# The head of a decoder layer: projections wait by weight quarter, the second chunk's queries and keys in front of the first's values, products of zeros in front, masks loaded last

## The chip, the cores and the metric

The kernel runs on one core of one Trainium2 chip. The time is that of the device for one execution, in microseconds (us); the measurement before is the median of three runs, 813.57 us (811.46 to 815.69). The engines are TensorE (PE in the profile; PEld is its weight load), VectorE (DVE), ScalarE (ACT), GpSimd (POOL) and SyncE (SP, which only issues DMAs here). A name with a q behind it (ACTq, SPq) is the instruction stream of that engine when it issues a DMA.

## The reference

A decoder layer in three blocks, each followed by a layer norm over `x + block(x)`, for 4 sequences of 512 tokens and 512 features. The first block, where the change lies, is linear attention:

```python
q = (x @ Wq).reshape(B, T, H, D)          # B = 4, T = 512, H = 16, D = 32, E = 512
k = (x @ Wk).reshape(B, T, H, D)
v = (x @ Wv).reshape(B, T, H, D)
q, k = _rotary(q), _rotary(k)
# chunks of 128 tokens: inter = (q * q_decay) @ kv, scores = (q @ k^T) * dmask, out = inter + scores @ v
attn = _rms_norm(attn, rms_w)             # x * rsqrt(mean(x * x) + eps) * w
return attn @ Wo
```

The second block is an int8-quantised gated product of each sequence with given weights, the third a gated feed-forward block whose weights are 4-bit codes with fp16 scales, decoded in the kernel.

## The kernel before, in words

**Tiling.** The 2048 tokens are 16 chunks of 128 (`CHUNKS`, four to a sequence). The attention block goes chunk by chunk. For chunk n: the tokens' features are transposed (`xT`, four 128x128 transposes on TensorE, L1266), projected to queries, keys and values (`q`, `k`, `v`, each one PSUM bank of 128x512), queries and keys are rotated by GpSimd (`rotate`), transposed per head group (`qT`, `kT`, L1302), the scores of 16 heads are formed (`s0` to `s3`, L1317), masked by VectorE (L1197), multiplied by the values (`attn`, L1345), and projected by Wo (`y`, L1362).

**Two parts per number.** Each float32 operand of a projection is split into a rounded part (`hi`, written by ScalarE) and the rest (`lo`, written by VectorE), and a product is three matmuls: hi with lo, hi with hi, lo with hi. So a projection of one chunk is 4 quarters (k = 0 to 3, 128 rows of the weight each) of 3 matmuls, 12 matmuls of 128x512 (L1278). The weights' own split happens once, at the head: `weight_hi(p)` on ScalarE (L959) and `weight_lo(p)` on VectorE (L1146), four instructions for each of Wq, Wk, Wv and Wo (p = 0 to 3). Each `lo` adds one to the semaphore `w_ready`. Wo is first multiplied by the norm's weights `rms_col` on VectorE (L1231), for which both must have landed (`wo_in`).

**Order.** Every engine has its own program, a list of instructions carried out in order, and waits on semaphores. The order of the uses of a PSUM bank is written out in `attention_order()`; q, k and v of chunk 0 lie in banks 2, 3 and 0, those of chunk 1 in the same banks after them. The streams at the head:

- SyncE issues x of chunk 0, the first halves of Wq and Wk, the table, the first half of Wv, the masks, the scales of the feed-forward weights, the packed words (`load_words(0)`, three DMAs, L896), then waits until all of Wo is split (`w_ready` at 16) and loads later inputs (L886, L913, L882).
- ScalarE first issues the identity, the second halves of Wq and Wk, x of chunk 1, the second half of Wv, all of Wo, and `rms_col`. Then it computes, in this order: `x_hi(0)`, `weight_hi(0)`, (1), (2), q and k of chunk 0 copied out of PSUM (`projected(0, 0)`, `projected(0, 1)`, L968), `x_hi(1)`, `projected(0, 2)`, `weight_hi(3)`, an fp16 identity (`ident16`, L1047), the scales' columns (L1049), and `chunk(0)`, which begins with q and k of chunk 1 and then `kT_hi` and `qT_hi`.
- VectorE: four small memsets, `x_lo(0)`, `weight_lo(0)`, (1), (2), `x_lo(1)`, the four multiplications of Wo, `weight_lo(3)`, then a wait for the table and the masks, and the chunks.
- TensorE: the transposes of chunk 0, then for p = 0 to 2 a wait until all four quarters of that weight are split and 12 matmuls, with the transposes of chunk 1 behind p = 1. Then `chunk(0)`: q of chunk 1, two fp16 transposing products of the scales that need `ident16` (`scale_columns`, L1288), k of chunk 1, the transposes of rotated q and k, the scores, and so on.
- GpSimd: rotates chunk 0 when its q and k have been copied out, writes the decayed keys `kd` of that chunk, then the same for chunk 1.

Of the kernel before, what the change touches and what calls it, by code (L numbers as in the profile page):

```python
# [19 lines left out]
P = 128  # L20
B, T, E = 4, 512, 512
NC = T // P
NK = E // P
H, D = 16, 32
HG = P // D
NG = H // HG
# [572 lines left out]
def attention_order():  # L599

    def pieces(n, place):
        return (("piece", m - len(PIECES)) for m in PIECES_AT.get((n, place), ()) if PIECE_BANKS[m] < 6)

    yield from (("xT", 0), ("q", 0), ("k", 0), ("xT", 1), ("v", 0), ("q", 1), ("k", 1))
    for n in range(CHUNKS):
        yield from (("qT", n), ("kT", n))
        if n > 0:
            yield from (("q", n + 1), ("k", n + 1))
        yield from (("s0", n), ("s1", n), ("s2", n), ("s3", n))
        if n % NC < NC - 1:  # L610
            yield ("kv", n)
        yield ("v", n + 1)
        yield from pieces(n, "masks")
        yield from (("attn", n), ("xT", n + 2))
        yield from pieces(n, "split")
        yield from (("y", n), ("ss", n))
        yield from pieces(n, "end")
# [144 lines left out]
def attention_programs(nc, sem, a, memory, expert, weights, x1, x2_v, x2_stored):  # L762
# [22 lines left out]
    z_first_loaded, z_loaded = sem("z_first_loaded"), sem("z_loaded")  # L785
    x1_first_stored, x1_stored = weights.x1_first_stored, weights.x1_stored
    words_in, bits_done, values_done = sem("words_in"), sem("bits_done"), sem("values_done")
    packed = sem("packed")
    ident_in, ident16_set, scales_in, scale_ps, cols_set = (sem("ident_in"), sem("ident16_set"), sem("scales_in"),
                                                            sem("scale_ps"), sem("cols_set"))  # L790
    wo_scaled = sem("wo_scaled")
# [88 lines left out]
    def sync_program(sp):  # L880
# [13 lines left out]
        def load_words(b):  # L894
            for dst, src in packed_words(b):
                sp.dma_start(dst, src).then_inc(words_in, 16)  # L896
# [3 lines left out]
        load_half(sp, 1, w_k, 0)  # L900
        sp.dma_start(tab[:, :], table[:, 2 * P:TABLE_W]).then_inc(tab_in, 16)
        load_half(sp, 2, w_v, 0)
        sp.dma_start(mask[:, :, :, :], masks.rearrange("p (j g c) -> p j g c", j=HG, g=NG)).then_inc(mask_in, 16)
        gu_rows, dn_rows = scale_rows[0:SCALES[0], 0, :], scale_rows[0:SCALES[1], 1, :]
        sp.dma_start(gu_rows, a["L0_ffn_gate_up_scales"].rearrange("g (t p) -> (g t) p", p=P)).then_inc(scales_in, 16)
        sp.dma_start(dn_rows, a["L0_ffn_down_scales"].rearrange("g (t p) -> (g t) p", p=P)).then_inc(scales_in, 16)
        load_words(0)
        sp.wait_ge(w_ready, 4 * NK)
        load_z(0, True)
        load_z(0, False)  # L910
# [29 lines left out]
    def scalar_program(act):  # L940
# [4 lines left out]
        load_half(act, 1, w_k, 1)  # L945
        act.dma_start(x_in[:, 1, :], x_v[0][:, 1, :]).then_inc(x_loaded[1], 16)
        load_half(act, 2, w_v, 1)
        act.dma_start(raw[:, 3], w_o.rearrange("(k p) n -> p k n", p=P)).then_inc(wo_in, 16)
        act.dma_start(rms_col[:, :], rms_w.rearrange("(k p) -> p k", p=P), allow_slow_non_contiguous=True)\
            .then_inc(wo_in, 16)  # L950

        def weight_hi(n):
            for k in range(NK):
# [7 lines left out]
        def x_hi(n):  # L961
            wait_full(act, "xT", n)
            nc.scalar.activation(xT_hi[:, n % 2], in_groups("xT", n), ACT.Copy).then_inc(xT_hi_done, 1)

        def projected(n, p):
            u = "qkv"[p]
            wait_full(act, u, n)
            nc.scalar.activation(qkv[:, n % 2, p * E:(p + 1) * E], bank(u, n)[:, :], ACT.Copy)\  # L968
                .then_inc(drain_sem(u, n), 1)
# [25 lines left out]

        def chunk(n):
            b, c = divmod(n, NC)
            if n == 0:
                projected(1, 0)
                projected(1, 1)  # L1000
            wait_full(act, "kT", n)
            nc.scalar.activation(kT_hi[:, :, :], in_groups("kT", n), ACT.Copy).then_inc(kT_hi_done, 1)
            wait_full(act, "qT", n)
# [33 lines left out]
        x_hi(0)  # L1037
        weight_hi(0)
        weight_hi(1)
        weight_hi(2)  # L1040
        projected(0, 0)
        projected(0, 1)
        x_hi(1)
        projected(0, 2)
        weight_hi(3)
        act.wait_ge(ident_in, 16)
# [72 lines left out]
    def vector_program(dve):  # L1119
# [58 lines left out]
        def chunk(n):  # L1178
# [41 lines left out]
            if n < CHUNKS - 1:  # L1220
                beside_pieces(weights.lo, dve, n, "end")

        expert.set_biases()
        x_lo(0)
        weight_lo(0)
        weight_lo(1)
        weight_lo(2)
        x_lo(1)
        dve.wait_ge(wo_in, 32)
        for k in range(NK):  # L1230
            nc.vector.tensor_scalar(raw[:, 3, k, :], raw[:, 3, k, :], rms_col[:, k:k + 1], None,  # L1231
# [16 lines left out]
    def tensor_program(pe):  # L1248
        steps = expert.tensor_steps(pe)

        def passes(lh, ll, rh, rl):

            return (lh, rl), (lh, rh), (ll, rh)
# [16 lines left out]
        def project(n, p, ks=range(NK)):  # L1270
            u = "qkv"[p]
            if ks[0] == 0:
                start_use(u, n)
                wait_drained(pe, "xT", n)
            for k in ks:
                for m, (lhs, rhs) in enumerate(passes(xT_hi[:, n % 2, k, :], xT_lo[:, n % 2, k, :],
                                                      wqkv_hi[:, p, k, :], wqkv_lo[:, p, k, :])):
                    last = nc.tensor.matmul(bank(u, n)[:, :], lhs, rhs, start=(k == 0 and m == 0),  # L1278
                                            stop=(k == NK - 1 and m == 2))
            if ks[-1] == NK - 1:  # L1280
                last.then_inc(full[BANK_OF[u]], 1)

        def scale_columns():
            pe.wait_ge(ident16_set, 1)
# [7 lines left out]
        def chunk(n):  # L1292
            c = n % NC
            if n == 0:
                project(1, 0)
                scale_columns()
                project(1, 1)
            pe.wait_ge(rot_done, 2 * (n + 1))
            for p, u in enumerate(("qT", "kT")):
                filled = start_use(u, n)  # L1300
# [69 lines left out]
            beside(steps, n, 2)  # L1370
            beside_pieces(weights.product, pe, n, "end")

        pe.wait_ge(ident_in, 16)
        transpose_x(0)
        for p in range(3):
            pe.wait_ge(w_ready, (p + 1) * NK)
            project(0, p)
            if p == 1:
                transpose_x(1)
        for n in range(CHUNKS):  # L1380
            chunk(n)

# [389 lines left out]
```

## Time and profile before

| | |
|---|---|
| median of 3 runs | 813.57 us (811.46 to 815.69) |
| the profiled execution's own time | 815.23 us |
| its span in the profile | 813.4 us |
| granted TensorE clock, mean | 0.961 |
| TensorE busy | 734.4 us (90%) |
| VectorE, ScalarE, GpSimd busy | 473.2, 354.7, 201.1 us |

The span runs from the first to the last instruction; the other 1.8 us of that execution's time lie around it. The profile rows give the start, the duration, engine, line and operation, then written tile `<-` read tiles, the shape and how many instructions are merged (`x4`); in brackets stands the idle time of the engine just before, and what ended it. TensorE's matmuls are pipelined, so a row's duration runs into the next row: what one costs in a series is the distance between two starts. The granted clock is given as a share of 2.4 GHz. In the first 12 us its column reads 1.00, though the distances there are those of 1.2 GHz.

### The profile page before, as it was taken

Reading aid. Unit: us, or ns where it says so; the run is one execution under the profiler, and the core shown is the slowest. Engines: PE = TensorE matmul, PEld = TensorE weight load, DVE = VectorE, ACT = ScalarE, POOL = GpSimd, SP = SyncE. Lnnn points to the kernel's source line nnn. Section 1 sums busy time; section 2 is a strip of 40 time slices with the busy share of each in tenths; the row PEclk is TensorE's granted clock in tenths of the full one; section 3 lists DMA queues with packets and bytes.
Section 4 is the critical chain, followed back from the end, with each engine's and each line's share of the span. In section 5 each row is a group of like instructions: output and inputs, shape, how many; then the busy total and the mean of one; then the engine's idle time right before and its main releaser. Section 6 shows DMA issues by size and latency. Waiting matters only on the chain.

```text
span 813.4 us, 11711 instructions
## 1 busy us (share of the span) xinstructions
PE 734.4 (90%) x4662; PEld 590.3 (73%) x4662; DVE 473.2 (58%) x911; ACT 354.7 (44%) x566; POOL 201.1 (25%) x235
## 2 busy tenths in 40 slices
PE   5898899998999898579899999999998999999992
PEld 4677678877887686358687777877777877788881
DVE  4566768783568656776625468655568454633214
ACT  4344454347453552462533463545364625522212
POOL 0444344344443459821201100211001111000000
PEclk9899999999999999759999999999999999999996
DMA  9400100102200220040001130030120030100201
GB/s 323 181 15 1 53 1 17 38 2 77 100 21 1 94 76 1 1 154 2 2 26 52 52 104 0 1 130 0 52 104 0 27 104 1 52 0 1 104 0 53
DMA packets 25408, 41.18 MB, mean 51 GB/s; under 512 B 5002, under 2 KB 7690, under 8 KB 25226
## 3 DMA queue, kind: packets, MB, share of 16 engines
q1 hardware_dynamic: 23194, 37.40, 13.5%
q10 hardware_dynamic: 2160, 3.02, 1.1%
q8 instruction: 38, 0.62, 0.3%
q14 instruction: 16, 0.13, 0.1%
HBM read 28.88 MB, written 11.53 MB: 50 GB/s over the span
## 4 chain that ended last, share of the span: by engine, by line
PE 59%; DVE 24%; ACT 10%; issue 2%; DMA 2%; POOL 1%; ACTq 0%; DVEq 0%; POOLq 0%
PE ps L1589 22%; PE ps L1278 11%; PE ps L1603 10%; PE ps L1362 3%; DVE small L413 3%; PE ps L1317 3%; PE ps L525 3%; PE ps L534 2%; DMA rms_col<-in_L_attn_rms_w_dram 2%; DVE masked L1197 2%; DVE w L406 2%; DVE act_s L374 2%; DVE act_s L406 1%; DVE weights L738 1%; PE ps L1345 1%
## 5 line engine op out<-in xcount | busy, mean ns | idle before, releaser
L1589 PE MATMUL ps<-x2T_hi,weights 128*128 128x512 f32 x704 | 220.0, 394 | 0.0
L1589 PEld LDWEIGHTS ps<-x2T_hi,weights 128*128 128x128 f32 x704 | 134.1, 191 | 27.9
L1589 PE MATMUL ps<-x2T_lo,weights 128*128 128x512 f32 x352 | 143.0, 406 | 0.8 <-DVE x2T_lo L1522 0.8
L1532 DVE TENSOR_TENSOR silu<-ps,silu 128x512 f32<-128x512 f32 x44 | 30.3, 689 | 147.5 <-PE ps L1589 147.5
L1603 PE MATMUL ps<-weights,h_hi 128*128 128x512 f32 x352 | 111.1, 397 | 1.8 <-DVE h_lo L1516 1.8
L1278 PE MATMUL ps<-wqkv_lo,xT_hi 128*128 128x512 f32 x192 | 81.9, 427 | 10.7 <-DVE wqkv_lo L1146 5.0
L1589 PEld LDWEIGHTS ps<-x2T_lo,weights 128*128 128x128 f32 x352 | 67.1, 191 | 15.1 <-DVE x2T_lo L1522 1.2
L1460 ACT ACTIVATE silu<-ps 128x512 f32<-128x512 f32 x44 | 26.3, 597 | 118.6 <-PE ps L1589 118.6
L1278 PE MATMUL ps<-wqkv_hi,xT_lo 128*128 128x512 f32 x192 | 77.1, 402 | 0.0
L1278 PE MATMUL ps<-wqkv_hi,xT_hi 128*128 128x512 f32 x192 | 77.1, 401 | 0.0
L1603 PEld LDWEIGHTS ps<-weights,h_hi 128*128 128x128 f32 x352 | 64.5, 188 | 15.1 <-DVE h_lo L1516 2.5
L1074 POOL TENSOR_TENSOR rot<-qkv,tab 128x256 f32<-128x256 f32 x64 | 44.7, 733 | 121.3 <-ACT qkv L968 121.3
L1454 ACT ACTIVATE h_hi<-silu 128x512 fp32r<-128x512 f32 x44 | 27.8, 631 | 103.0 <-DVE silu L1532 103.0
L1603 PE MATMUL ps<-weights,h_lo 128*128 128x512 f32 x176 | 68.7, 390 | 0.0
L338 POOL TENSOR_SCALAR act_s<-act_s 128x1024 f32<-128x1024 f32 (+1 forms) x16 | 13.3, 830 | 183.3 <-ACT act_s L276 183.2
L1197 DVE TENSOR_TENSOR masked<-ps,mask 128x512 f32<-128x512 f32 x64 | 39.7, 683 | 28.9 <-PE ps L1317 28.9
L1278 PEld LDWEIGHTS ps<-wqkv_lo,xT_hi 128*128 128x128 f32 x192 | 37.2, 194 | 21.7 <-DVE wqkv_lo L1146 5.4
L1516 DVE TENSOR_TENSOR h_lo<-silu,h_hi 128x512 fp32r<-128x512 f32 x44 | 30.6, 696 | 37.4 <-ACT h_hi L1454 37.4
L968 ACT ACTIVATE qkv<-ps 128x512 f32<-128x512 f32 x48 | 28.6, 596 | 53.4 <-PE ps L1278 53.3
L1278 PEld LDWEIGHTS ps<-wqkv_hi,xT_lo 128*128 128x128 f32 x192 | 37.3, 194 | 8.6
L1278 PEld LDWEIGHTS ps<-wqkv_hi,xT_hi 128*128 128x128 f32 x192 | 37.3, 194 | 6.4
L1603 PEld LDWEIGHTS ps<-weights,h_lo 128*128 128x128 f32 x176 | 33.0, 188 | 7.2
(170 smaller groups left out, 1357.5 us busy)
## 6 DMA issues: line engine op xcount, KB each, us to landing
w<-in_fside_BxS2xS_dram SPq DMA_DIRECT2D x4, 1024.0 KB, 5.3
x_dram<-xb SPq DMA_DIRECT2D x4, 1024.0 KB, 4.3
xc<-x_dram SPq DMA_DIRECT2D x4, 1024.0 KB, 5.5
x_in<-in_x_dram SPq DMA_DIRECT2D x15, 256.0 KB, 3.4
xb<-x_dram SPq DMA_DIRECT2D x3, 1024.0 KB, 5.6
out_dram<-xc SPq DMA_DIRECT2D x3, 1024.0 KB, 4.7
z<-in_x_dram SPq DMA_DIRECT2D x3, 768.0 KB, 5.2
x_dram<-z SPq DMA_DIRECT2D x3, 768.0 KB, 3.5
```

What stands on the lines that cost most here:

```text
L406: step = nc.vector.tensor_tensor(act_s[:, c, 0:width] if use[0] in "xa" else src[:, c, 0:width], src[:, c, 0:width], self.bank(use)[:, 0:w ...
L413: then_wait(nc.vector.tensor_reduce(small[:, slot, :], src[:, :, 0:width], AX.X, ALU.max, apply_absolute_value=True))
L968: nc.scalar.activation(qkv[:, n % 2, p * E:(p + 1) * E], bank(u, n)[:, :], ACT.Copy)\
L1074: nc.gpsimd.tensor_tensor(rot[:, m], v, f, ALU.mult).then_inc(rot_a, 1)
L1197: nc.vector.tensor_tensor(masked[:, j], in_groups(f"s{j}", n), mask[:, j], ALU.mult)\
L1278: last = nc.tensor.matmul(bank(u, n)[:, :], lhs, rhs, start=(k == 0 and m == 0), stop=(k == NK - 1 and m == 2))
L1454: nc.scalar.activation(h_hi[:, it % 2, :], silu[:, it % 2, :], ACT.Copy).then_inc(h_hi_done, 1)
L1460: nc.scalar.activation(silu[:, it % 2, :], ps[4][:, :], ACT.Silu).then_inc(silu_done, 1)
L1516: nc.vector.tensor_tensor(h_lo[:, it % 2, :], silu[:, it % 2, :], h_hi[:, it % 2, :].bitcast(F32), ALU.subtract).then_inc(h_lo_done, 1)
L1532: nc.vector.tensor_tensor(silu[:, it % 2, :], ps[5][:, :], silu[:, it % 2, :], ALU.mult)\
L1589: last = nc.tensor.matmul(dst[:, :], lhs, rhs, start=(k == 0 and n == 0), stop=(k == NK - 1 and n == 2))
L1603: last = nc.tensor.matmul(ps[c][:, :], lhs, rhs, start=(it == 0 and n == 0), stop=(it == NI - 1 and n == 2))
```

## The change

It has five parts, all at the head.

1. TensorE's first projections wait quarter by quarter (`w_ready` at p * 4 + k + 1 in front of quarter k), for chunk 0 alone.
2. q and k of chunk 1 are projected in front of v of chunk 0, on TensorE, in the order of bank uses and on ScalarE; ScalarE's split of Wv goes behind `x_hi(1)`, VectorE's `x_lo(1)` in front of `weight_lo(2)`.
3. VectorE sets one half of `kd` (128x512) to zero first of all; TensorE multiplies its columns by one another, 14 times in front of the transposes of chunk 0 and 10 times behind them, into a bank that nothing reads (`turn_over`).
4. The loads of Wo and `rms_col` go from ScalarE's stream to SyncE's, in the place of the masks.
5. The load of the masks goes behind the packed words.

```diff
-    yield from (("xT", 0), ("q", 0), ("k", 0), ("xT", 1), ("v", 0), ("q", 1), ("k", 1))
+    yield from (("xT", 0), ("q", 0), ("k", 0), ("xT", 1), ("q", 1), ("k", 1), ("v", 0))
@@ sync_program
         load_half(sp, 2, w_v, 0)
-        sp.dma_start(mask[:, :, :, :], masks.rearrange("p (j g c) -> p j g c", j=HG, g=NG)).then_inc(mask_in, 16)
+        sp.dma_start(raw[:, 3], w_o.rearrange("(k p) n -> p k n", p=P)).then_inc(wo_in, 16)
+        sp.dma_start(rms_col[:, :], rms_w.rearrange("(k p) -> p k", p=P), allow_slow_non_contiguous=True)\
+            .then_inc(wo_in, 16)
...
         load_words(0)
+        sp.dma_start(mask[:, :, :, :], masks.rearrange("p (j g c) -> p j g c", j=HG, g=NG)).then_inc(mask_in, 16)
@@ scalar_program
         load_half(act, 2, w_v, 1)
-        act.dma_start(raw[:, 3], w_o.rearrange("(k p) n -> p k n", p=P)).then_inc(wo_in, 16)
-        act.dma_start(rms_col[:, :], rms_w.rearrange("(k p) -> p k", p=P), allow_slow_non_contiguous=True)\
-            .then_inc(wo_in, 16)
...
         def chunk(n):
             b, c = divmod(n, NC)
-            if n == 0:
-                projected(1, 0)
-                projected(1, 1)
...
         weight_hi(1)
-        weight_hi(2)
         projected(0, 0)
         projected(0, 1)
         x_hi(1)
+        weight_hi(2)
+        projected(1, 0)
+        projected(1, 1)
         projected(0, 2)
         weight_hi(3)
@@ vector_program
+        nc.vector.memset(kd[:, 1, :], 0.0).then_inc(zeros_set, 1)
         expert.set_biases()
         x_lo(0)
         weight_lo(0)
         weight_lo(1)
+        x_lo(1)
         weight_lo(2)
-        x_lo(1)
@@ tensor_program
             for k in ks:
+                if n == 0:
+                    pe.wait_ge(w_ready, p * NK + k + 1)
...
+        def turn_over(times):
+
+            for _ in range(times):
+                nc.tensor.matmul(ps[7][:, 0:P], kd[:, 1, 0:P], kd[:, 1, P:2 * P], start=True, stop=True)
...
             if n == 0:
-                project(1, 0)
                 scale_columns()
-                project(1, 1)
...
+        pe.wait_ge(zeros_set, 1)
+        turn_over(14)
         pe.wait_ge(ident_in, 16)
         transpose_x(0)
-        for p in range(3):
-            pe.wait_ge(w_ready, (p + 1) * NK)
-            project(0, p)
-            if p == 1:
-                transpose_x(1)
+        turn_over(10)
+        project(0, 0)
+        project(0, 1)
+        transpose_x(1)
+        project(1, 0)
+        project(1, 1)
+        project(0, 2)
```

## Rows read from the trace of the kernel before

**Rows 1.** The page: busy time and share of TensorE, VectorE, ScalarE, GpSimd.

```profile
PE 734.4 (90%) x4662; PEld 590.3 (73%) x4662; DVE 473.2 (58%) x911; ACT 354.7 (44%) x566; POOL 201.1 (25%) x235
```

**Rows 2.** Chain of waits, 3 to 25 us: start, duration, what.

```profile
3.85 16.96 DMA rms_col<-in_L_attn_rms_w_dram
...
20.83 3.51 DVE raw L1231 x4
...
24.36 0.63 ACT wo_hi L959
```

**Rows 3.** TensorE in order of time, 4 to 32 us.

```profile
4.34 1.11 PE L1266 MATMUL ps<-ident_ones,x_in 128*128 128x128 f32 x4 [4.34 <-DMA ident_ones<-in_table_dram]
10.50 0.79 PE L1278 MATMUL ps<-wqkv_lo,xT_hi 128*128 128x512 f32 x1 [5.05 <-DVE wqkv_lo L1146]
...
15.35 0.40 PE L1278 MATMUL ps<-wqkv_hi,xT_lo 128*128 128x512 f32 x1
...
18.32 0.60 PE L1266 MATMUL ps<-ident_ones,x_in 128*128 128x128 f32 x4
18.67 0.48 PE L1278 MATMUL ps<-wqkv_lo,xT_hi 128*128 128x512 f32 x1
...
24.00 0.39 PE L1278 MATMUL ps<-wqkv_hi,xT_lo 128*128 128x512 f32 x1
25.25 0.34 PE L1288 MATMUL ps<-sq 88*128 88x88 f16 x2 [0.86 <-ACT sq L1047]
...
28.39 1.03 PE L1302 MATMUL ps<-ident_ones,qkv 128*128 128x128 f32 x8
31.70 0.34 PE L1317 MATMUL ps<-qT_lo,kT_hi 32*128 32x128 f32 x4 [2.27 <-DVE qT_lo L1184]
```

**Rows 4.** ScalarE in order of time, 3 to 28 us, and 362 to 368 us.

```profile
3.85 1.55 ACTq L949 DMA_DIRECT2D rms_col<-in_L_attn_rms_w_dram  x1
5.43 1.28 ACT L963 ACT_TABLE_LOAD   x1 [5.43 <-issue]
6.72 0.60 ACT L963 ACTIVATE xT_hi<-ps 128x512 fp32r<-128x512 f32 x1
7.22 2.18 ACT L959 ACTIVATE wqkv_hi<-raw 128x512 fp32r<-128x512 f32 x4
...
362.77 1.28 ACT L1460 ACT_TABLE_LOAD   x1
367.34 0.60 ACT L1460 ACTIVATE silu<-ps 128x512 f32<-128x512 f32 x1 [3.29 <-PE ps L1589]
```

**Rows 5.** VectorE in order of time, 0 to 31 us.

```profile
0.81 0.15 DVE L258 MEMSET biases<- 128x1 f32 x4 [0.81 <-PEq L1758]
...
7.96 5.08 DVE L1146 TENSOR_TENSOR wqkv_lo<-raw,wqkv_hi 128x512 fp32r<-128x512 f32 x8
```

**Rows 6.** SyncE's stream, 4 to 28 us.

```profile
4.61 9.93 SPq L896 DMA_DIRECT2D halves<-_ffn_gate_up_packed_dram  x3
```

**Rows 7.** TensorE in order of time: products of 128x128 at either clock.

```profile
33.86 2.08 PE L1326 MATMUL ps<-qkv,kd 128*128 128x128 f32 x8
35.59 0.77 PE L1278 MATMUL ps<-wqkv_lo,xT_hi 128*128 128x512 f32 x1
...
52.62 1.16 PE L1326 MATMUL ps<-qkv,kd 128*128 128x128 f32 x8
53.53 0.48 PE L1278 MATMUL ps<-wqkv_lo,xT_hi 128*128 128x512 f32 x1
...
325.50 2.08 PE L1338 MATMUL ps<-qdT,kv 128*128 128x128 f32 x8
...
357.64 3.65 PE L1621 MATMUL ps<-ident_ones,xb 128*128 128x128 f32 x16 [1.87 <-DVE weights L738]
```

**Rows 8.** Stretches: us, length, busy of the five engines, granted clock, DMA share, GB/s.

```profile
32.30:39.10 6.80, 6.80 (x66) 5.60 (x65) 3.08 (x5) 0.00 (x0) 2.32 (x3) 0.51 1.02 381
...
329.00:330.00 1.00, 0.99 (x18) 0.45 (x8) 0.00 (x0) 0.49 (x1) 1.00 (x2) 0.82 0.00 0
```

More of the change, by code:

```diff
@@ L787, in attention_programs @@
     words_in, bits_done, values_done = sem("words_in"), sem("bits_done"), sem("values_done")
-    packed = sem("packed")
+    packed, zeros_set = sem("packed"), sem("zeros_set")
     ident_in, ident16_set, scales_in, scale_ps, cols_set = (sem("ident_in"), sem("ident16_set"), sem("scales_in"),
```

## The prediction

> **What bounds the kernel now.** I read the page's first part, then the chain of waits, then each engine in order of time over the first 40 us, because all edits lie there. The first shows TensorE busy for 90% of the span with no other engine above 58% [rows 1]: outside the head TensorE carries the time, and whatever the head gains or loses is handed on nearly whole. The chain begins with the load of `rms_col`, which follows that of Wo and is in after 20.81 us; then come the multiplications of Wo on VectorE, the split of Wo on ScalarE, the fp16 identity, and the scales' products on TensorE at 25.25 [rows 2, 3]. On TensorE I mark three losses. It does nothing but four transposes before 10.50, where the first projection had waited 5.05 us for the whole split of Wq. From 10.50 to about 15.2 a matmul of 128x512 costs 0.43 us, which is 1.2 GHz; from 15.35 on 0.23, which is 2.4 GHz. And it stands for 0.86 us in front of the scales' products [rows 3]. The mark I measure by is the start of the transposes of rotated q and k at 28.39 [rows 3]: all that the change reorders lies in front of it, and from it on the programs are the same.
>
> **The first projection.** The zeroing is put in front of VectorE's first instruction at 0.81 [rows 5]. No row shows a memset of 128x512; the nearest are the memset of 128x1, 0.15 us, and the split of 128x512, 5.08 / 8 = 0.64 [rows 5]. I take 0.6, since the size decides, so products begin at about 1.5 (1.0 to 1.6). A float32 product of 128x128 costs (35.59 - 33.86) / 4 = 0.43 us at 1.2 GHz and (53.53 - 52.62) / 4 = 0.23 at 2.4 [rows 7]. Fourteen are 6.0 us at the low clock, more than the 2.8 us left until the identity lands at 4.34 [rows 3], so they delay the transposes. How much depends on when the clock rises. Before, it rose some 4.7 us after the first projection [rows 3]; the same distance here gives 6.2. By then (6.2 - 1.5) / 0.43 = 10.9 products are done, the other 3.1 take 0.7: 6.9. The transposes end at 7.5 (0.60 us as at 18.32 [rows 3]) instead of 5.45.
>
> ScalarE was not ready at 5.45 either: its stream issued DMAs until 5.40, then loaded its table for 1.28, and `xT_hi` began at 6.72 [rows 4]. Two of those DMAs leave its stream (1.55 for `rms_col` and about 0.55 for Wo), so the table load can begin at about 3.3. Does it run before the wait for TensorE is over? At 362.77 it did: the load ran at once and its activation waited 3.29 us more [rows 4]. So it ends at 4.6, hidden, and `xT_hi` starts at 7.55, which is 0.83 later than before; were it not hidden, 1.28 more. The first quarter of Wq's `lo` came 7.96 + 0.64 - 6.72 = 1.88 after `xT_hi` [rows 4, 5], thus at 9.45. The ten products behind the transposes run from 7.25 to 9.6. First projection: **9.6** instead of 10.50, all at the high clock.
>
> Do the waits by quarter cost or bring anything? VectorE delivers a quarter every 0.64 us [rows 5], TensorE needs 3 x 0.232 = 0.70 (23 distances in the 5.33 us from 18.67 to 24.00 [rows 3]), so behind the first quarter none is waited for; the waits earn only that the first matmul starts behind the first quarter, not the fourth, and that is inside the 9.6. The last quarter of Wk is there at 13.9 and wanted at 14.5.
>
> **From there to the mark.** q and k of chunk 0: 24 matmuls at the high clock, 5.55, end at 15.15 (before: 7.82 us, of which 2.27 are lost to the low clock [rows 3]). Transposes of chunk 1: 0.35, until 15.5. Now q of chunk 1 stands next, and it needs `xT_lo` of chunk 1: behind the copy of k (from 15.35, 0.5), `xT_hi` (0.65) and `xT_lo` (0.7) it is there at 17.25. Before, v of chunk 0 filled that gap; now TensorE waits **1.75 us**. Wv's split behind it is in time: ScalarE from 16.35 to 18.5, VectorE to about 19.7, wanted at 22.8. Three projections, 36 x 0.23 = 8.3, end at **25.55**.
>
> Here the gain is lost. ScalarE copies v of chunk 0 only now (25.75), and `weight_hi(3)` stands behind that copy in its list. Before, that copy ran at 21.7, and the Wo split was limited by the landing [rows 2]. Now the landing is no limit: the products of Wo by `rms_col` would be done by about 24.3 even with the landing at 20.8, yet the split runs from 26.25, four times 0.53 (rate of Wq's, 2.18 for four with overlap [rows 4]), to 28.35; the fp16 identity is ready so that the scales' products start at 28.7 (0.89 after the start of the last split, 24.36 to 25.25 [rows 2, 3]), after a wait of 3.15 us. With 0.26 for them the mark is at **28.96, 0.57 later** than 28.39. Check by differences: start -0.9, low clock -2.27, new gap +1.75, last wait 3.15 instead of about 1.0 (24.23 to 25.25) +2.15, rest -0.15: +0.6.
>
> Bounds of this part: a rise of the clock at 4.9 lets the products end early and the first projection come at about 9.0, mark at +0.0; a rise only at 8.9 moves the transposes' end to 8.6 and the first projection to 10.9, mark at +1.8; a table load that isn't hidden, +1.1.
>
> **The clock behind the mark.** Before, TensorE stood from 29.4 to 31.70, its clock fell at 32.3 and rose at 39.1, so 6.8 us passed at half speed [rows 3, 8]. Now, from 25.55 to the scores at about 32.3, it has 0.26 us of products and 1 us of transposes. The clock falls again, and probably earlier: the 8 transposes then take 1.86 instead of 0.93 and the scores 2.6 instead of 2.2. I add **0.9**, between nothing and 1.3, and keep 3 more us at the high end for a second such stretch.
> What the trace shows of transposes: sixteen filled 3.65 us from 357.64 on and the clock stayed at 0.5 [rows 7]. The Trainium skill, TensorE: Matmul & The Clock Gate, Part 4 (PE-mode transpose), says that transposes don't count as busy for the clock gate. By that rule nearly the whole 6.7 us count as idle and the sum is the one above; were they to count, the 0.9 would go. The trace agrees with the rule.
>
> **What costs nothing.** The masks are issued behind the packed words, whose three issues last until 14.5 [rows 6], somewhat later with 1.55 us for `rms_col` and the 0.5 for Wo ahead. VectorE waits for the masks in front of `kT_lo`, at about 30.8; the bytes of the head are the same, and were all in at 20.8 [rows 2], so some 9 us cover it. SyncE's wait for `w_ready` ends some 1.5 us later, with it the loads behind; the transposes of chunk 2 that need x are 1.5 later as well. GpSimd rotates chunk 0 some 3 us earlier and chunk 1 some 6 us earlier, and neither was waited for.
>
> **Sum.** 0.57 + 0.9 = +1.5 on the execution of 815.23 us: 816.7. That one lies 1.7 above the median of the runs, 813.57, to which I add the same: **815.1 us**.
>
> **Rivals.**
> *The products of zeros don't raise the clock.* For it: from 32.3 to 35.7 TensorE was full with scores and four such products and stayed low to 39.1 [rows 7, 8]. Against: the clock rose near 329.2 after such products from 325.50 on and small ones behind them, with none of 128x512 in 5 us before [rows 7, 8]. Then all 24 run at 0.43 with slow transposes between: 1.5 + 6.0 + 1.1 + 4.3 = 12.9 for the first projection, +2.4; no low clock is saved, 0; gap and last wait +1.75 + 2.15, rest -0.15: +6.2, with 0.9 behind the mark +7.1: **820.7 us**. It decides from the point where fewer than half of the products run at the high clock. Chance 0.14.
> *The clock doesn't fall behind the mark.* The 6.8 us [rows 8] would shrink: scores 0.7, `kd` products 0.8, six projection matmuls 1.4, values 0.3, together 3.2, against +0.6: -2.6, **811.0 us**. Against it speaks the long idle before the scores. Chance 0.12.
> *The wait for Wo stays as before.* If DMAs in SyncE's stream land Wo after 25 us, the multiplications (3.51 [rows 2]) set the split: every us beyond 22.7 costs one. A landing at 25 gives +2.3 more, **817.4 us**. The queue behind it held back three issues for 9.9 us [rows 6], Wo stands in front of them. Chance 0.06.
>
> **How the numbers follow.** My forecast holds 0.68. Range: from 811.0, the case in which the clock stays, to 819.5, past the late-rise and late-Wo cases and part of the way to 820.7. 0.5% is 4.1 us, about what a measurement of this kernel tells from no change (three runs spread over 4.2). Faster by more needs the clock to stay and a lucky early rise: 0.07. Slower by more: the zeros rival and a part of the others, 0.17. Within: 0.76.
>
> **What would show it.** Right: first L1278 near 9.6 and starts 0.23 apart at once; a gap of some 1.7 us in front of q of chunk 1; L1288 at 28 to 29.5 behind ScalarE's split of Wo, which starts behind the copy of v; transposes at 29 to 30; half clock from before 32. Wrong: L1288 without a wait, or transposes before 27, would mean that the gain isn't eaten; starts 0.43 apart beyond 12 us, that the zeros don't work; a `masked` that waits for the masks, that the cover in the DMA part is gone.

## The result, and the profile after

| | before | changed |
|---|---|---|
| median, 16 runs each | 814.86 us (811.46 to 817.48) | 817.71 us (815.94 to 821.01) |
| ratio to before, 95% interval | | 1.0040 (1.0025 to 1.0054) |
| profiled execution, its span | 815.23, 813.4 us | 817.66, 815.8 us |
| granted clock of that execution, mean | 0.961 | 0.955 |

The change makes the kernel slower by 0.4%, some 3 us, less than the 0.5% that I had named as the bound, though with 16 runs of each the interval lies wholly above 1. The forecast was 815.1 us (811.0 to 819.5), a rise of 1.5. So the measured 817.71 lies inside the range and 2.6 us above its middle: 1.3 us of that because the kernel before is at 814.86 over 16 runs, not at the 813.57 of the three runs that I started from, and the other 1.3 because the rise was some 3 us and not 1.5.

TensorE of the changed kernel in order of time, columns as in [rows 3]. L1288 are the products of zeros (28 records for 14 products), L1280 the projections (before L1278), L1295 the scales' products, L1307 the transposes of queries and keys, L1322 the scores:

```profile
1.45 4.91 PE L1288 MATMUL ps<-kd 128*128 128x128 f32 x28 [1.45 <-DVE kd L1222]
6.20 0.60 PE L1266 MATMUL ps<-ident_ones,x_in 128*128 128x128 f32 x4
6.64 2.40 PE L1288 MATMUL ps<-kd 128*128 128x128 f32 x20
8.90 0.47 PE L1280 MATMUL ps<-wqkv_lo,xT_hi 128*128 128x512 f32 x1
...
14.47 0.60 PE L1266 MATMUL ps<-ident_ones,x_in 128*128 128x128 f32 x4
16.62 0.47 PE L1280 MATMUL ps<-wqkv_lo,xT_hi 128*128 128x512 f32 x1 [1.55 <-DVE xT_lo L1149]
...
24.66 0.39 PE L1280 MATMUL ps<-wqkv_hi,xT_lo 128*128 128x512 f32 x1
28.00 0.34 PE L1295 MATMUL ps<-sq 88*128 88x88 f16 x2 [2.96 <-ACT sq L1046]
28.27 1.73 PE L1307 MATMUL ps<-ident_ones,qkv 128*128 128x128 f32 x8
32.34 0.48 PE L1322 MATMUL ps<-qT_lo,kT_hi 32*128 32x128 f32 x4 [2.33 <-DVE qT_lo L1183]
```

From top to bottom: the first projection starts 1.60 us earlier than in [rows 3]; queries and keys of chunk 0 are done 3.85 us earlier (14.47 against 18.32); then come two holes, 1.55 us in front of the queries of chunk 1, and 2.96 us in front of the scales' products; the mark, the transposes of queries and keys, stands at 28.27 against 28.39. Of 3.85 us there are 0.12 left. The second hole is explained by ScalarE's list:

```profile
22.36 0.60 ACT L968 ACTIVATE qkv<-ps 128x512 f32<-128x512 f32 x1 [2.12 <-PE ps L1280]
25.08 0.60 ACT L968 ACTIVATE qkv<-ps 128x512 f32<-128x512 f32 x1 [2.12 <-PE ps L1280]
25.57 2.18 ACT L959 ACTIVATE wo_hi<-raw 128x512 fp32r<-128x512 f32 x4
27.65 0.30 ACT L1046 ACTIVATE sq<-ident_ones 128x128 f16<-128x128 f32 x1
```

The second row is the copy of the values of chunk 0. ScalarE waits 2.12 us for it with nothing to do, and only then splits Wo, for which everything had been ready since 24.2 (the multiplications by `rms_col` run on VectorE from 20.75 for 3.42 us).

Stretches of the changed kernel, columns as in [rows 8]; the first answers to the low stretch there:

```profile
28.00:39.00 11.00, 8.66 (x72) 7.64 (x72) 7.02 (x10) 1.37 (x3) 1.43 (x2) 0.53 0.66 231
39.00:62.00 23.00, 20.81 (x202) 16.75 (x200) 14.20 (x31) 9.13 (x12) 9.31 (x11) 1.00 0.19 63
62.00:70.00 8.00, 5.91 (x18) 4.80 (x19) 5.43 (x12) 5.23 (x7) 2.78 (x3) 0.57 0.00 0
70.00:103.00 33.00, 30.38 (x293) 25.17 (x290) 21.37 (x42) 11.02 (x17) 12.52 (x16) 1.00 0.12 30
103.00:108.00 5.00, 3.82 (x11) 3.07 (x12) 3.52 (x11) 3.56 (x5) 1.80 (x2) 0.66 0.06 21
```

and three of these of the kernel before:

```profile
28.00:39.00 11.00, 8.73 (x85) 7.20 (x87) 4.37 (x7) 1.68 (x3) 5.21 (x7) 0.70 0.92 332
62.00:70.00 8.00, 6.70 (x28) 5.59 (x29) 5.92 (x13) 5.57 (x9) 2.79 (x3) 0.79 0.00 0
103.00:108.00 5.00, 5.00 (x29) 4.26 (x28) 2.80 (x8) 4.14 (x6) 1.80 (x2) 1.00 0.00 0
```

The granted clock (the third number from the end) is lower in three places: 0.53 for 0.70, 0.57 for 0.79, 0.66 for 1.00. The way of the loss: 0.12 us ahead at the mark, 0.64 behind at the scores (32.34 against 31.70), 0.79 at Wo's product of chunk 0 (42.45 against 41.66), 1.79 at the transposes of chunk 2's queries (69.59 against 67.80), 3.09 at those of chunk 4 (108.50 against 105.41), 2.4 at the end of the span.

### The profile page after: what moved, and what is told of

Same layout as the page of the kernel before. It is cut to its first block, busy times and chain, and to the rows that moved or that the text cites. A ratio compares the mean times of both kernels' runs of the same rounds, so it can differ in the third digit from the quotient of the medians.

```text
span 815.8 us, 11808 instructions
## 1 busy us (share of the span) xinstructions
PE 741.7 (91%) x4710; PEld 598.0 (73%) x4710; DVE 476.3 (58%) x912; ACT 354.4 (43%) x566; POOL 203.2 (25%) x235
## 4 chain that ended last, share of the span: by engine, by line
PE 60%; DVE 24%; ACT 10%; issue 2%; POOL 1%; DMA 1%; SPq 0%; DVEq 0%; ACTq 0%; POOLq 0%
PE ps L1598 22%; PE ps L1280 12%; PE ps L1612 10%; PE ps L1367 3%; DVE small L413 3%; PE ps L525 2%; PE ps L1322 2%; PE ps L534 2%; DVE masked L1196 2%; DVE w L406 2%; DVE act_s L374 1%; DVE act_s L406 1%; DVE weights L738 1%; DVE e_stats L459 1%; ACT values_gu L980 1%
## 5 line engine op out<-in xcount | busy, mean ns | idle before, releaser
L1280 PE MATMUL ps<-wqkv_lo,xT_hi 128*128 128x512 f32 x192 | 80.8, 421 | 7.2 <-ACT rms L1029 2.8
L1280 PE MATMUL ps<-wqkv_hi,xT_lo 128*128 128x512 f32 x192 | 76.1, 397 | 0.0
L1280 PE MATMUL ps<-wqkv_hi,xT_hi 128*128 128x512 f32 x192 | 76.0, 396 | 0.0
L1280 PEld LDWEIGHTS ps<-wqkv_lo,xT_hi 128*128 128x128 f32 x192 | 36.6, 191 | 17.8 <-issue 4.7
L1280 PEld LDWEIGHTS ps<-wqkv_hi,xT_lo 128*128 128x128 f32 x192 | 36.6, 191 | 8.4
L1280 PEld LDWEIGHTS ps<-wqkv_hi,xT_hi 128*128 128x128 f32 x192 | 36.8, 192 | 6.3
```

## The experiments

Each kernel was timed beside the kernel before on the same chip, in three series of four (e1 to e4, e5 to e8, e9 to e12), each series on another chip, with 5 to 12 runs for each kernel and 23 to 28 of the kernel before. The changed kernel was not timed again in them; its row is from the result above. "Mark" is the start of the transposes of queries and keys of chunk 0, "y" that of Wo's product of chunk 0, in the one profiled execution. The profiled executions of e1 and e3 are quicker than their medians (811.67 and 806.91 us); I read positions in the head from them, no times. A position moves between executions too: up to the mark the kernel before and e5 differ only by two small loads that nothing waits for there, and their marks are 0.9 us apart (28.39 and 29.29), so a difference of less than a microsecond at the mark or at y says little. The median of the kernel before was 814.94, 816.43 and 816.11 us in the three series, so ratios are compared across them, not medians.

| kernel | median us | ratio to before (95%) | mark | y |
|---|---|---|---|---|
| changed | 817.71 | 1.0040 (1.0025 to 1.0054) | 28.27 | 42.45 |
| e1: Wo's split ahead | 816.03 | 1.0011 (0.9984 to 1.0037) | 25.89 | 40.63 |
| e2: without products of zeros | 820.65 | 1.0074 (1.0046 to 1.0101) | 30.97 | 46.55 |
| e3: old order of projections | 813.14 | 0.9979 (0.9958 to 1.0000) | 26.00 | 37.55 |
| e4: e1 and 8 products behind the mark | 819.72 | 1.0063 (1.0042 to 1.0085) | 26.10 | 41.98 |
| e5: before, x loaded early | 815.76 | 0.9985 (0.9970 to 1.0000) | 29.29 | 40.95 |
| e6: e1, x loaded early | 816.16 | 0.9991 (0.9977 to 1.0006) | 26.45 | 40.25 |
| e7: e3, x loaded early | 811.58 | 0.9936 (0.9920 to 0.9952) | 25.60 | 37.29 |
| e8: e4, x loaded early | 813.42 | 0.9954 (0.9940 to 0.9968) | 26.21 | 38.92 |
| e9: e7 and the 8 products | 810.71 | 0.9943 (0.9918 to 0.9969) | 25.41 | 35.76 |
| e10: before, new loads alone | 813.94 | 0.9979 (0.9960 to 0.9997) | 26.93 | 39.96 |
| e11: e9 and 14 products in chunk 1 | 807.27 | 0.9892 (0.9860 to 0.9924) | 25.91 | 36.26 |
| e12: e7, one wait per weight | 812.50 | 0.9956 (0.9937 to 0.9976) | 27.14 | 38.88 |

**Is it the place of Wo's split (e1)?**

```diff
-        projected(0, 2)
         weight_hi(3)
         act.wait_ge(ident_in, 16)
         nc.scalar.activation(ident16, ident, ACT.Copy).then_inc(ident16_set, 1)
+        projected(0, 2)
```

> The changed kernel with one thing moved: ScalarE's split of Wo and the fp16 identity in front of its copy of v of chunk 0. My theory (the gain of the head is lost because that split stands behind the copy of v): no wait of 3 us in front of the scales' products, transposes of q and k at 25.4 instead of 28.3, scores of chunk 0 at 28.8 instead of 32.3, the time 3 us below the changed kernel's, so about level with the kernel before or 0.5 under it. Rival (the loss lies behind the mark, in the clock, and takes whatever the head gives): transposes at 25.4 too, but the values' part of chunk 0 as late as in the changed kernel and its time as well, 817 to 818.

```profile
25.31 0.34 PE L1295 MATMUL ps<-sq 88*128 88x88 f16 x2 [0.25 <-ACT sq L1045]
25.89 1.06 PE L1307 MATMUL ps<-ident_ones,qkv 128*128 128x128 f32 x8 [0.24 <-ACT qkv L968]
30.14 0.48 PE L1322 MATMUL ps<-qT_lo,kT_hi 32*128 32x128 f32 x4 [3.19 <-DVE qT_lo L1183]
...
40.22 0.66 PE L1266 MATMUL ps<-ident_ones,x_in 128*128 128x128 f32 x4 [0.96 <-DMA x_in<-in_x_dram]
```

At the mark the theory holds: 0.25 us of wait instead of 2.96, and the mark 2.38 us earlier. The time followed by 1.7 us, not 3, and the ratio's interval overlaps that of the changed kernel: by itself the time doesn't settle it. The rows show where the rest stays. The wait in front of the scores grew from 2.33 to 3.19, because VectorE is busy with the rest of Wo's split when `kT_hi` is ready. And TensorE now waits for x of chunk 2, which it did not in the kernel before.

**Do the products of zeros pay (e2)?** Part 3 is left out: `turn_over`, its calls and the memset.

> The changed kernel without the 24 products of zeros and without the zeroing. Theory (the products pay for themselves by the clock, 2.3 us, and cost part of that by delaying the transposes and the first projection): first projection at 7.9 instead of 8.9 but 0.43 us a matmul until about 12.5, projection of k of chunk 0 done at 15.8 instead of 14.6, transposes of q and k at 29.5 instead of 28.3, time +1 us against the changed kernel. Rival (the products are a net loss): projection of k done before 14.6 and the time lower by 1 us.

Without them k of chunk 0 ended 2.67 us later (17.14 against 14.47) and so did the mark, 2.70. The median is 2.9 us higher, more than the 1 us that I expected. The two intervals overlap a little (1.0046 to 1.0101, and 1.0025 to 1.0054), but six of the seven runs without the products lie above 15 of the 16 with them. I had the first projection at 7.9 where it came at 8.69: the split of Wq waits for its landing until 7.19, so without the products it is that landing that bounds the start, and the delay of the transposes by the products cost only 0.2 us. So they lose next to nothing of what the clock brings. How much that is, is partly chance: here the low clock lasted 6.1 us from the first projection, in [rows 3] 4.7.

**Is it the order of projections (e3)?** Part 2 is undone on all engines, the rest of the change is kept.

> The changed kernel with the order of projections of the kernel before on all engines (v of chunk 0 in front of q and k of chunk 1, the split of Wv in front of the copies, the split of Wo between them), with waits by quarter, zeros and new load order kept. Theory (the new order of projections is what costs): v of chunk 0 fills the gap of 1.55 us in front of q of chunk 1, the scales' products wait less than 1 us, transposes of q and k at 25.5, time 3 us below the changed kernel's. Rival (the order costs nothing, the loads or the clock do): transposes near 28 and the time that of the changed kernel.

```profile
14.50 0.60 PE L1267 MATMUL ps<-ident_ones,x_in 128*128 128x128 f32 x4
15.78 0.47 PE L1281 MATMUL ps<-wqkv_lo,xT_hi 128*128 128x512 f32 x1 [0.68 <-DVE wqkv_lo L1146]
...
22.87 0.34 PE L1296 MATMUL ps<-sq 88*128 88x88 f16 x2 [1.12 <-ACT sq L1047]
26.00 1.03 PE L1310 MATMUL ps<-ident_ones,qkv 128*128 128x128 f32 x8
29.30 0.33 PE L1325 MATMUL ps<-qT_lo,kT_hi 32*128 32x128 f32 x4 [2.27 <-DVE qT_lo L1184]
```

Two holes of 4.5 us together are now two of 1.8 (0.68 and 1.12), the mark is 2.27 us earlier, the scores 3.04. The ratio falls from 1.0040 to 0.9979 with intervals apart: **the new order costs 0.6%, about 4.6 us** (817.71 less 813.14, with the two medians of before 0.1 apart), and the other four parts together are worth 0.2%, with an interval that touches 0. Here the theory and the time agree.

**Is the idle behind the mark what drops the clock (e4)?**

```diff
+        def hold(times):
+            for _ in range(times):
+                nc.tensor.matmul(ps[7][:, 0:P], ident, ones, start=True, stop=True)
...
                 step.then_inc(filled, 1)
+            if n == 0:
+                hold(8)
```

> The first of these (Wo's split ahead of the copy of v), and 8 products of identity by ones behind the transposes of q and k of chunk 0, where TensorE stands for 2.3 us until the scores. Theory (transposes don't count for the clock and the wait behind them does, so the clock falls in front of the scores): the clock stays high through the scores and values of chunk 0, which saves 2 to 3 us more: values of chunk 0 done 5 to 6 us earlier than in the changed kernel, time 5 us below it. Rival (the fall has another cause, or it is chance of the moment): half clock from the scores on all the same, and the time that of the first, plus up to 1 us where the products run at half clock and delay the scores.

A miss: the slowest but one. The first two rows below went as I wanted, eight products in the idle and the scores at the high clock (their groups 0.11 us apart). But the clock fell all the same, only later: the stretch from 32.6 to 35.8 has a granted clock of 0.50, so the low stretch behind the mark is 3.4 us long where it was 6.8 in e1. The last row shows the price:

```profile
27.00 1.95 PE L1292 MATMUL ps<-ident_ones 128*128 128x128 f32 x16
30.37 0.33 PE L1328 MATMUL ps<-qT_lo,kT_hi 32*128 32x128 f32 x4 [1.42 <-DVE qT_lo L1183]
35.82 1.12 PE L1356 MATMUL ps<-masked,qkv 128*32 128x128 f32 x32
41.57 0.66 PE L1266 MATMUL ps<-ident_ones,x_in 128*128 128x128 f32 x4 [3.03 <-DMA x_in<-in_x_dram]
```

TensorE arrives 2 us sooner and waits 3.03 us for x of chunk 2. Soon behind that wait, from 42.8 on, its clock is low again, and Wo's product takes 4.4 us (41.98 to 46.40) instead of 2.8 in e1. SyncE's list shows why x is late: five loads of 3 MB together stand before it, and those wait for Wo's split.

```profile
28.99 0.81 SPq L886 DMA_DIRECT2D xb<-in_x_dram  x2
29.84 0.96 SPq L886 DMA_DIRECT2D z<-in_x_dram  x2
30.84 0.49 SPq L916 DMA_DIRECT2D w<-in_fside_BxS2xS_dram  x1
31.38 11.21 SPq L882 DMA_DIRECT2D x_in<-in_x_dram  x3
```

**Is x of chunk 2 the next limit (e5 to e8)?** Four kernels get the same edit. It does two things: x of chunks 2 and 3 is loaded in front of SyncE's wait for the split of Wo, and the second sequence's residual loads (`load_z(1, ...)`) wait until the first's have landed. No run has one without the other:

```diff
+        for n in range(2):
+            wait_full(sp, "xT", n)
+            load_x(n + 2)
         sp.wait_ge(w_ready, 4 * NK)
         load_z(0, True)
         load_z(0, False)
-        load_z(1, True)
-        load_z(1, False)
         sp.dma_start(expert.w[:, :, :], w_rows[0]).then_inc(expert.w_in, 16)
+        sp.wait_ge(z_first_loaded, 16)
+        sp.wait_ge(z_loaded, 16)
+        load_z(1, True)
+        load_z(1, False)
...
             if n + 2 < CHUNKS:
-                wait_full(sp, "xT", n)
-                load_x(n + 2)
+                if n >= 2:
+                    wait_full(sp, "xT", n)
+                    load_x(n + 2)
```

> The kernel before with x of chunks 2 and 3 loaded as soon as their buffers are read, in front of SyncE's wait for the split of Wo, and the second sequence's residual loads behind the first's landing. In the trace of the kernel before nothing waited for x of chunk 2, so by my theory (this load is a limit only once the head is quicker than in the kernel before) the time is that of the kernel before within 1 us. Rival (the load order costs in every case): 1 to 2 us less.

> The changed kernel with Wo's split ahead of the copy of v, and the early loads of x of chunks 2 and 3. Theory (x of chunk 2, issued behind the split of Wo and five large loads, is the next limit): the wait of 0.96 us for it is gone, the transposes of the second chunk's queries at 42.6 instead of 43.6, time 1 us below that of the kernel with Wo's split ahead alone (816.0). Rival (that wait only stood beside another of the same length): both marks as there, time 816.

> The changed kernel with the old order of projections, and the early loads of x. Theory as in the one before: the wait of 1.0 us for x of chunk 2 gone, transposes of the second chunk's queries at 39.6 instead of 40.5, time 1 us below the old order's 813.1, so some 812, 3 us under the kernel before. Rival: 813.

> The kernel with Wo's split ahead and 8 products of identity by ones behind the transposes, with the early loads of x. Without them it was slower (819.7) than its twin without products (816.0), and in its trace TensorE waited 3.03 us for x of chunk 2 and ran at half clock for 3.4 us behind that wait. Theory (the products do hold the clock; the time that they gain ends at x of chunk 2, and the wait there drops the clock again): the wait and the half clock at 42 to 46 are gone, transposes of the second chunk's queries at 41 instead of 46.5, time near 814, 5 us below 819.7. Rival (the products themselves cost the time): 819 again.

None of the four waits for x of chunk 2. In the kernel before (e5) it brought at most 0.3%, with an interval that touches 1. With Wo's split ahead (e6) no clear gain, though y is 0.4 earlier in an execution whose first projection was 0.55 later: 0.9991 against 1.0011, intervals overlapping. With the old order (e7) the ratio went from 0.9979 to 0.9936, intervals just apart, and with the products (e8) from 1.0063 to 0.9954: a loss of 0.6% turned into a gain of 0.5%. Against e6, its twin without the 8 products in the same series, e8 is 2.7 us quicker with the intervals apart. So the products behind the mark are worth something, and in e4 the late loads took it and more. As in e4, they shorten the low stretch behind the mark (3.4 us in e8, 6.8 in e6) and don't remove it. Rows of e8, in order of time:

```profile
27.12 1.95 PE L1298 MATMUL ps<-ident_ones 128*128 128x128 f32 x16
30.57 0.33 PE L1334 MATMUL ps<-qT_lo,kT_hi 32*128 32x128 f32 x4 [1.50 <-DVE qT_lo L1189]
38.56 0.60 PE L1272 MATMUL ps<-ident_ones,x_in 128*128 128x128 f32 x4
...
41.89 1.07 PE L1317 MATMUL ps<-ident_ones,qkv 128*128 128x128 f32 x8
```

**What the parts are worth, and what they give together (e9 to e12).** e9 is e7 with the 8 products; e10 the kernel before with parts 4 and 5 alone; e12 is e7 with the waits of the kernel before in place of part 1; e11 is e9 with this:

```diff
             beside_pieces(weights.product, pe, n, "split")
+            if n == 1:
+                hold(14)
```

> The changed kernel with the old order of projections, the early loads of x, and 8 products of identity by ones behind the transposes of chunk 0's queries and keys. It joins what gained alone (old order with early loads 811.6; products with the split of Wo ahead 813.4 against 816.2 without them). Theory (they act in different places: the order at the mark, the products on the clock behind it): no low clock between 20 and 55 us, time 2 us below the old order's with early loads, so near 809.5. Rival (the old order leaves so short an idle that the clock's fall there costs nothing): 811.5.

> The kernel before with the new places of the loads alone: Wo and rms_col in SyncE's stream in the masks' place, the masks behind the packed words. Theory (Wo lands some 3 us earlier, the split of Wo and the identity are done sooner, the wait of 0.86 us in front of the scales' products goes, and the first copy starts 1.2 us earlier because ScalarE's stream is shorter): first projection at 9.3 to 10.5, transposes of queries and keys at 26.5 to 27.5 instead of 28.4, time 1 to 2 us below the kernel before. Rival (the loads give nothing, since a wait for one thing is replaced by the next): transposes at 28.4 and the time of before.

> The kernel with old order, early loads and 8 products, and 14 more products of identity by ones in front of Wo's product of chunk 1, where TensorE waits 4.2 us for VectorE and ScalarE. Theory (the idle of 4.2 us is what drops the clock at 60 us, for 3.4 to 6.8 us): no low clock before 95 us, transposes of the third chunk's queries 4.5 us behind y of chunk 1's start in low-clock traces become 3 us, time 1.5 to 2.5 us below its twin without the 14. Rival (the clock falls all the same, or the products delay Wo's product): the same time or 1 us more.

> The changed kernel with old order and early loads, but with one wait per weight, as in the kernel before, instead of one per quarter. Theory (VectorE delivers a quarter each 0.64 us, TensorE needs 0.70, so the quarters save what lies between the first and the fourth quarter minus what the products of zeros hide): first projection 1.0 to 1.5 us later, transposes of queries and keys later by that or less, time up to 1 us above 811.6. Rival (the first projection is bound by the products in front, not by the quarters): no difference.

e10: the new loads alone bring 0.2% (0.03 to 0.40) and 1.46 us at the mark. `xT_hi` starts at 5.20 instead of 6.72, the wait in front of the scales' products is 0.25, and TensorE now waits 1.12 us for x of chunk 2. The ratio, 0.9979, is that of e3, which has the waits by quarter and the products of zeros on top of these loads: without the early loads of x, no time shows that parts 1 and 3 add anything to parts 4 and 5. e12: TensorE waits 1.67 us for all of Wq. Its twin for comparison is e9 rather than e7, because in both the fourteen products in front lasted until 7.59 and `xT_hi` started at 8.26, and up to the mark their programs differ by the waits alone: the first projection comes 1.81 us later (12.13 against 10.32), the mark 1.73 (27.14 against 25.41). The times of e12 and e7 (0.9956 against 0.9936) don't tell them apart. e9: no low clock from 20 to 55 us, y 1.5 us earlier than in e7, but the clock fell for 6.8 us at 55, and the time is only 0.9 us lower in series with different medians of before; not told apart from e7. That fits e3 and e7, whose low clock behind the mark was none and 3.4 us: with the old order there is little there to hold. e11 takes that next fall away; the first low stretch of its trace begins at 196 us. TensorE of e11, then its stretches:

```profile
53.52 3.29 PE L1299 MATMUL ps<-ident_ones 128*128 128x128 f32 x28
57.97 0.50 PE L1384 MATMUL ps<-wo_lo,o_hi 128*128 128x512 f32 x1 [1.16 <-DVE o_lo L1218]
...
60.98 1.07 PE L1320 MATMUL ps<-ident_ones,qkv 128*128 128x128 f32 x8
```

```profile
28.00:39.00 11.00, 10.38 (x123) 8.60 (x122) 7.61 (x18) 3.09 (x6) 6.43 (x9) 1.00 0.78 283
39.00:62.00 23.00, 21.84 (x199) 18.89 (x198) 15.42 (x32) 10.85 (x13) 9.75 (x12) 1.00 0.01 2
62.00:70.00 8.00, 8.00 (x82) 6.67 (x81) 5.06 (x9) 2.66 (x6) 1.69 (x3) 1.00 0.00 0
103.00:108.00 5.00, 5.00 (x69) 4.22 (x68) 2.49 (x10) 0.81 (x3) 2.11 (x4) 1.00 0.02 5
```

The clock stays at 1.00 in all four, Wo's product of chunk 1 takes 2.9 us (57.97 to 60.84; 64.09 to 69.37 in the changed kernel), and the time is 807.27 us, **1.1% (0.8 to 1.4) below the kernel before**: the best of all. Against its twin e9 that is 3.4 us; with five runs the two intervals still touch (0.9860 to 0.9924, 0.9918 to 0.9969), but in the same series every run of e11 (805.68 to 808.14) is quicker than every run of e9 (809.54 to 812.71).

## Why the prediction was right, point by point

The path was right: the head's gain is lost at Wo's split and at the new gap, and the clock costs about 0.9 us more behind the mark. The size was not: the middle was low by 2.6 us, and it would have been further off if the start of the head, forecast 0.7 us too late, had not made up for a part of the low stretches that the sum left out. That much of the agreement is luck.

- *The first projection.* Right in kind, 0.7 us too late: 8.90 for 9.6. The zeroing took 0.48 us, not 0.6, and 14 products from 1.45 to 6.20 are 4.75 us: with 0.43 and 0.23 us each that makes 7.6 slow ones and a rise of the clock at about 4.7. I had put it at 6.2; 4.9 was my lower bound, and the mark came out a little below the bound that went with it (-0.12 for +0.0). The table load ran ahead of the wait as read from [rows 4] (3.25 to 4.5, then 2.30 us idle).
- *The waits by quarter.* That they cost nothing is shown by the distances of 0.23 from the first matmul on; e12 against e9 puts their worth at 1.7 us at the mark, in one execution each and with the old order of projections.
- *The gap in front of q of chunk 1.* 1.55 for 1.75.
- *The gain is lost at Wo's split.* 2.96 us of wait for 3.15, the split starting behind the copy of the values as written down. e1 and e3 remove it, each in another way, and each moves the mark by more than 2.2 us. Mark at 28.27 for 28.96, the 0.7 us of the first projection.
- *The clock behind the mark, +0.9.* Transposes 1.73 us for 1.86, scores from the first at half clock. From mark to y the changed kernel lost 0.79 + 0.12 = 0.91. The test by which I took the rule on transposes to agree with the trace was weak: sixteen of them at the low clock for 3.65 us show little when projections took 4.7 us in [rows 3] before the clock rose. No run here separates the transposes from the waits around them.
- *The step that was too small* is that I priced no second low stretch in the sum and only kept it at the high end. At chunk 1 TensorE waits 4.2 us in both kernels; Wo's product behind that wait took 4.35 us in the profiled execution of the kernel before (the first two rows) and 5.3 in that of the changed one:

```profile
63.30 0.79 PE L1362 MATMUL ps<-wo_lo,o_hi 128*128 128x512 f32 x1 [4.21 <-DVE o_lo L1212]
67.65 0.28 PE L1368 MATMUL ps<-ident_ones,sq 128*128 128x1 f32 x2
```

```profile
64.09 0.80 PE L1367 MATMUL ps<-wo_lo,o_hi 128*128 128x512 f32 x1 [4.21 <-DVE o_lo L1211]
69.37 0.35 PE L1373 MATMUL ps<-ident_ones,sq 128*128 128x1 f32 x2
```

  A third stretch came at 103, behind a wait of 2.98 us that the kernel before has too, without a fall of its clock. The two cost 1.0 and 1.3 us; 0.7 of that is made up later, which leaves 1.6 of the 2.4 us of span. e11 shows that the stretch at chunk 1 can be taken away. Why the changed kernel falls longer there is not shown. Chance of the moment plays a part: behind the same wait of 4.2 us the low stretch is 3.4 us long in six of the profiled executions (before, e1, e3, e5, e8, e10) and 6.8 in seven (changed, e2, e4, e6, e7, e9, e12), and kernels with the same order of projections stand in both lists. Against mere chance speaks that its 16 runs have mean granted clocks of 0.955 to 0.959, while 15 of the 26 runs of the kernel before in the third series lie above 0.959. Those runs are from different chips. Which of the shifts does it stays open.
- *What costs nothing.* The masks cost nothing: issued at 15.44, never waited for. The loads behind Wo's split were nearly uncovered: x of chunk 2 landed at 42.0 where TensorE wanted it at 41.8. I had said that the loads and these transposes would both move by 1.5 us. SyncE's wait ended 3.1 us later (30.68 against 27.61) and the transposes came 0.7 later (42.04 against 41.31), so the cover was used up. In e1 and e4 it was the limit.
- *What I had not seen.* VectorE's split of Wo took 4.43 us (26.23 to 30.66), where it took 3.34 in the kernel before. GpSimd rotates chunk 1 in that stretch, where in the kernel before it worked only for the first microsecond. The four instructions that split Wv show the same more clearly. First the changed kernel, where GpSimd rotates chunk 0 beside them, then e3, where GpSimd starts when they are done:

```profile
15.44 3.68 POOL L1073 TENSOR_TENSOR rot<-qkv,tab 128x256 f32<-128x256 f32 x4 [15.00 <-ACT qkv L968]
16.39 4.43 DVE L1145 TENSOR_TENSOR wqkv_lo<-raw,wqkv_hi 128x512 fp32r<-128x512 f32 x4
```

```profile
14.94 2.50 DVE L1146 TENSOR_TENSOR wqkv_lo<-raw,wqkv_hi 128x512 fp32r<-128x512 f32 x4 [1.79 <-ACT wqkv_hi L959]
17.62 3.16 POOL L1074 TENSOR_TENSOR rot<-qkv,tab 128x256 f32<-128x256 f32 x4 [17.18 <-ACT qkv L968]
```

  So a quarter takes 1.11 us beside a working GpSimd and 0.63 without. No run changes GpSimd alone, but nothing else that the rows show differs: ScalarE's part was done at 17.8 and was not waited for. Rotating earlier is thus not free, though I had assumed that it is: 1.1 of the 3.1 us by which SyncE's loads moved is the longer split of Wo. The split of Wo ended at 30.66, just as `kT_hi` did, and cost TensorE nothing here, but 0.9 us in e1.
- *Rivals.* That the zeros don't raise the clock is refuted (0.23 us distances from 8.90; without them, in e2, 0.43 until about 14.8). That the clock stays behind the mark: it fell at 28 already. That Wo lands late: it was in at about 17, earlier than before.

## What to carry to other kernels

Before moving work forward on the bound engine, write down for each engine what stands in its list between the moved work's new neighbours: here the copy of a late product came to stand in front of work that had been ready, and a gain of 3.85 us was gone at the next meeting point. Where a gain does not arrive, look for a load whose issue waits in a long queue: the next limit was a small load of 256 KB behind 3 MB that nobody needed yet. And a long wait of the matmul engine can cost twice, once by itself and once by the half clock of what follows it: the wait of 4.2 us at chunk 1 did so in all 13 traces that have it, the one of 2.98 us at 102 in some and not in others. Products into an unused bank, placed inside waits that can't be removed and sized to end before them, brought 2.7 us behind the mark (e8 against e6) and 3.4 at chunk 1 (e11 against e9), where the reordering cost 4.6. They pay only if the next wait isn't one for a load: in e4 the same products made the kernel 3.7 us slower than e1. Last, before moving work to an earlier place on an engine that is not the bound, look at what runs beside it.

## What the runs showed of the hardware

- Products of zeros raise the clock: float32 products of 128x128 with both operands zero took it from 1.2 to 2.4 GHz, at about 4.7 us in the changed kernel; in the executions of e9 and e12 all fourteen ran at the low clock, until 7.59. The moment differs between executions by some 3 us.
- The issue of the small scales' load (22 KB) held SyncE's stream for 5.09 us in the changed kernel, and the three issues of the packed words behind it took 5.65, in the same place in which [rows 6] has 9.93 us for the words alone; the masks' issue moved to 15.44 for it.
- The time of one kernel and its mean granted clock go together: in the third series, eleven runs of the kernel before at 0.958 or 0.959 average 816.8 us, three at 0.966 or above 811.9 (809.34, 811.25, 815.0).
- VectorE's split of one 128x512 quarter took 0.61 to 0.64 us while GpSimd stood still, and 1.11 us on average while GpSimd rotated (the split of Wv in the changed kernel, e1, e2, e4, e6 and e8).
